# One-hots of a graph attention layer: half of them stored by the score stage and loaded back by the message stage

## The reference, cut to what matters

```python
def gt_layer(x, ntype, etype, src, dst, Wk, Wq, Wv, Wa, Watt, Wmsg, pri, skip, g, b):
    ...
    kT = jnp.einsum('nhd,htdo->nhto', k, Watt)
    vT = jnp.einsum('nhd,htdo->nhto', v, Wmsg)
    kw = kT[src, :, etype]
    m = vT[src, :, etype]
    a = jnp.einsum('ehd,ehd->eh', kw, q[dst]) * pri[:, etype].T / SQRT_D
    att = edge_softmax(a, dst, n)
    msg = (m * att[:, :, None]).reshape(-1, H * HS)
    hag = jax.ops.segment_sum(msg, dst, num_segments=n)
    ...
```

## Time and profile before

| | us |
|---|---|
| median of three executions | 5878.2 |
| the profiled execution | 5883.0 |
| its span, first to last instruction | 5881.1 |
| score stage of the first attention layer, first product store to last sum | 3807.7 to 4296.4 |
| message stage of the first attention layer, first load to last matmul | 4405.8 to 4528.7 |
| message stage of the second attention layer | 5591.0 to 5714.2 |

### The profile page before, as it was taken

The page is one execution under the profiler, slowest core; times in us unless marked ns, Lnnn a source line. Parts: engine busy times, 40 slices in busy tenths (PEclk is TensorE's granted clock), DMA queues, the critical chain, the costliest instruction groups (busy, mean ns, idle before and its releaser), DMA issues. The chain is left out here.

```text
span 5881.1 us, 64328 instructions
## 1 busy us (share of the span) xinstructions
PE 3437.1 (58%) x15913; PEld 2664.7 (45%) x15913; DVE 2302.7 (39%) x4944; ACT 1099.9 (19%) x2255; POOL 3190.0 (54%) x3405
## 2 busy tenths in 40 slices
PE   2777677767757777544654436555526265555272
PEld 2777555545546775433343322244416222444162
DVE  6222333343343334311221134444476444444774
ACT  0000222232231112000100003311116133111162
POOL 0777577667747773777377732177711320777102
PEclk9555688888875556655655567765659677565595
DMA  1222244434434333222322139955516499555162
GB/s 39 53 53 53 74 123 123 116 99 121 123 81 120 105 107 106 65 53 53 135 56 53 53 118 399 359 160 162 162 41 196 138 389 375 160 162 162 43 200 64
DMA packets 600862, 772.39 MB, mean 131 GB/s; under 512 B 89654, under 2 KB 506920, under 8 KB 587984
## 3 DMA queue, kind: packets, MB, share of 16 engines
q1 hardware_dynamic: 479920, 492.16, 25.0%
q0 software_dynamic: 120608, 276.12, 17.9%
HBM read 416.10 MB, written 351.82 MB: 131 GB/s over the span
## 5 line engine op out<-in xcount | busy, mean ns | idle before, releaser
L395 POOL DMA_INDIRECT arena<-table,idx_s x3128 | 2968.2, 949 | 1743.9 <-issue 903.0
L632 PE MATMUL ps<-arena,onehot 128*128 x4160 | 1056.8, 400 | 672.3 <-POOLq L391 638.6
L632 PEld LDWEIGHTS ps<-arena,onehot 128*128 128x128 f32 x4160 | 848.3, 284 | 807.5 <-issue 807.3
L373 DVE TENSOR_TENSOR onehot<-ps,dl_s 128x512 f32<-128x512 f32 x520 | 355.4, 685 | 813.0 <-PE ps L632 777.5
L1722 PE MATMUL ps<-ident,onehot 128*128 128x128 f32 x832 | 207.1, 396 | 438.5 <-DVE onehot L373 433.5
L1682 DVE TENSOR_TENSOR arena<-arena,ps 128x128 f32<-128x128 f32 x832 | 183.9, 282 | 560.0 <-POOLq L391 461.2
L1733 PE MATMUL ps<-arena 128*128 x1664 | 382.0, 404 | 9.4 <-issue 7.4
L802 DVE SCALAR_TENSOR_TENSOR arena<-ps,vecs,arena 128x256 f32<-128x256 f32 x208 | 100.5, 483 | 677.3 <-ACT arena L781 671.3
L1722 PEld LDWEIGHTS ps<-ident,onehot 128*128 128x128 f32 x832 | 135.5, 199 | 493.2 <-DVE onehot L373 487.4
L1733 PEld LDWEIGHTS ps<-arena 128*128 128x128 f32 x1664 | 335.8, 300 | 44.8 <-issue 40.6
L1602 PE MATMUL ps<-arena,XT 32*128 32x512 f32 x1600 | 305.0, 891 | 67.6 <-DVE XT L1626 42.8
(11 more groups left out here) (324 smaller groups left out, 4426.6 us busy)
## 6 DMA issues: line engine op xcount, KB each, us to landing
table<-arena SPq DMA_DIRECT2D x96, 2048.0 KB
values<-arena SPq DMA_DIRECT2D x832, 64.0 KB
arena<-values SPq DMA_DIRECT2D x208, 256.0 KB
arena<-table,idx_s POOLq DMA_INDIRECT x3128
arena<-edge_times SPq DMA_DIRECT2D x208, 128.0 KB, 3.4
edge_part<-arena SPq DMA_DIRECT2D x208, 128.0 KB
table<-arena SPq DMA_DIRECT2D x50, 512.0 KB
arena<-edge_part SPq DMA_DIRECT2D x98, 256.0 KB, 2.9
```

The costliest lines, as they stand in the source:

```text
L373: is_dst = dve.tensor_tensor(onehot[:, 4 * q:4 * q + 4, :], iota.unsqueeze(1).to_broadcast([P, 4, P]), dl_s[:, ds(j, 4)].unsqueeze(2).to_b ...
L395: pool.indirect_dma_start(ring[:, ds(t % RING * 2 * H, width)], None, tab, bass.IndirectOffsetOnAxis(ap=idx_s[:, t:t + 1], axis=0)).then_i ...
L632: mm = pe.matmul(accf[:, ds(b, P)], o, ring[:, ds(slot, H)], start=False, stop=False, skip_group_check=True)
```

## The change

The one-hots of the even quads (0 and 2 of each trip), which VectorE makes in the score stage anyway, are stored to a DRAM tensor `marks` there (52 stores of 256 KB per layer, in rows of 2 KB) and loaded back into the same places of `onehot` in the message stage (52 loads per layer). VectorE makes none in the message stage.

```diff
+        marks = dram("marks", [ALL_QUADS // 2, P, 4 * P])
...
+        mark_out = [signal(f"mark_out{u}") for u in range(2)]
+        mark_in = [signal(f"mark_in{u}") for u in range(2)]
...
-        def onehots(dve, weight, after=None, iota=None):
+        def onehots(dve, weight, after=None, iota=None, guard=None):
...
                     if not first:
                         dve.wait_ge(quad_done.sem, quad_done.at(n - 3))
+                        if guard is not None:
+                            guard(i, q)
...
# score_phase, SyncE
+                                if q % 2 == 0:
+                                    sp.wait_ge(onehot_ready.sem, onehot_ready.at(n + 1))
+                                    sp.dma_start(marks[n // 2, :, :], onehot[:, 4 * q:4 * q + 4, :].rearrange("p s d -> p (s d)")).then_inc(mark_out[q // 2].sem, 16)
                         trips(sp, body)
...
+                        for u in range(2):
+                            sp.wait_ge(mark_out[u].sem, mark_out[u].at(16 * TRIPS))
...
# score_phase, VectorE
+                        def kept(i, q):
+                            if q % 2 == 0:
+                                dve.wait_ge(mark_out[q // 2].sem, mark_out[q // 2].at(16 * i))
+                        onehots(dve, None, lagged, iota=ps[:, 2, 0:P], guard=kept)
...
# message_phase, SyncE
                             for q in range(QUADS):
+                                if q % 2 == 0:
+                                    if not first:
+                                        sp.wait_ge(quad_done.sem, quad_done.at(i * QUADS + q - 3))
+                                    sp.dma_start(onehot[:, 4 * q:4 * q + 4, :].rearrange("p s d -> p (s d)"),
+                                                 marks[(i * QUADS + q) // 2, :, :]).then_inc(mark_in[q // 2].sem, 16)
                                 if not first:
                                     sp.wait_ge(mixed.sem, mixed.at(i * QUADS + q - 3))
                                 sp.dma_start(vals[:, 4 * q:4 * q + 4, :],
...
# message_phase, VectorE
-                                if q % 2 == 0:
-                                    dve.tensor_tensor(onehot[:, 4 * q:4 * q + 4, :], iota_row[:, :].unsqueeze(1).to_broadcast([P, 4, P]),
-                                                      dl_s[:, ds(j, 4)].unsqueeze(2).to_broadcast([P, 4, P]), ALU.is_equal).then_inc(onehot_ready.sem, 1)
...
# message_phase, TensorE
                                 if q % 2 == 0:
-                                    pe.wait_ge(onehot_ready.sem, onehot_ready.at(i * 2 + q // 2 + 1))
+                                    pe.wait_ge(mark_in[q // 2].sem, mark_in[q // 2].at(16 * (i + 1)))
```

More of the change, by code:

```diff
@@ L1696, in lagged @@
                                 reduce(i if q >= 3 else i - 1, (q - 3) % QUADS)
-                        onehots(dve, None, lagged, iota=ps[:, 2, 0:P])
+                        def kept(i, q):
+                            if q % 2 == 0:
+                                dve.wait_ge(mark_out[q // 2].sem, mark_out[q // 2].at(16 * i))
+                        onehots(dve, None, lagged, iota=ps[:, 2, 0:P], guard=kept)
                         for q in range(QUADS - 2, QUADS):
@@ L1752, in score_phase @@
                     s.base += 64 * TRIPS
+                for s in mark_out:
+                    s.base += 16 * TRIPS
             def softmax_phase():
@@ L1921, in message_phase @@
                 mixed.base += ALL_QUADS
-                onehot_ready.base += 2 * TRIPS
                 evac.base += 2 * TRIPS
                 squared.base += HALF * TRIPS
+                for s in mark_in:
+                    s.base += 16 * TRIPS
                 for s in ring_in[0:QUADS]:
```

## The result

The changed kernel takes 5987.5 us (median of four executions, 5981.7 to 5989.3), the kernel before on the same chip 5878.4 us: a ratio of 1.0183, 95% interval 1.017 to 1.0195, so 109 us slower. Forecast were 5982 us and a range of 5922 to 6030.

What follows compares the result with a forecast made beforehand. GpSimd was taken to bound the score stage, with four nearly full resources in the message stage. A new load loop and slower clock add 101 us, score stages 3: 5878.2 + 104 = 5982 us, range 5922 to 6030.

Steps and rivals of the forecast that it cites:

- The new loop: Message stage: marks' load waits for TensorE's quad n-4 with values behind it on SyncE; 6.16 us a trip against 4.52.
- the clock: TensorE in the message stage: a fifth of the time at 1.2 GHz, lengthening the trip from 6.16 to 6.47 us.
- the sign that I had named for being wrong: Message stage: TensorE's granted clock staying 1.00 would show the forecast wrong, with 5967 us instead.
- The engines' 5.34 us: Message stage: transfer engines need 3.61 + 1.73 us a trip for values and marks; no trip can go below.
- The score stage: GpSimd's pace hides the marks' stores and VectorE's wait; only 1.4 us shows at its end, 3 us for both layers.
- rival D: Score stage: marks' stores hold up the gathers for their whole length, +89 us on top, 6071 us; 3%.
- B: Message stage: loads hidden and VectorE's relief shows, -27 us, 5851 us; 4%, half of it faster, half no change.
- A: Message stage: values land as fast as a lone load and the clock holds, 5.37 us a trip, 5925 us; 12%.
- C: Message stage: values land as a burst's fourth, a third of the time at low clock, 7.32 us a trip, 6027 us; 20%.
- VectorE's 4.12 us a trip: Message stage before the change: VectorE's work per trip, 4 x 0.689 + 2 x 0.684 us.
- That sum, 104 us: Whole kernel: 101 us from 52 longer message-stage trips and 3 us from the score stages, added to the median.

Runs made afterwards that it cites:

- The wait alone: Kernel before plus SyncE's wait for TensorE to finish quad n-4 before loading an even quad's values, no marks: 5929.2 us, ratio 1.008.
- The bytes alone: Changed kernel, but marks loaded into unread places without waiting for TensorE, and VectorE still makes the one-hots: 5919.3 us, ratio 1.0064.
- values first: Changed kernel with SyncE issuing both quads' values before the marks and their wait; slower chips: 7107.6 us, ratio 1.0099; repeated 7101.7 us, 1.0089.
- half the bytes: Changed kernel with each marks load bringing two of four matrices (128 KB), waits and order kept; slower chip: 7132.4 us, ratio 1.0124.

## Why the prediction was right

**The new loop was the right step.** Forecast were 6.16 us a trip from the loop and 6.47 with the clock; measured 6.33 and 6.51. The wait alone gave 5.40 us with no byte added, and taking the values out from behind the wait, with the same bytes, brought 5.75 and 5.72 on a queue of their own, and 5.32 when they were issued first (on the slower chips, stages alone compared).

**One term was undersized, another oversized, and they met.** The terms of the loop, forecast and taken from the trace of the changed kernel (us, means of 48 turns per stage, from the third trip on):

| term | forecast | first stage | second stage |
|---|---|---|---|
| TensorE's end to the marks' issue | 0.02 | 0.03 | 0.03 |
| marks' issue to the values' issue | 0.46 | 0.38 | 0.39 |
| values' issue until VectorE uses them | 3.60 | 3.83 | 3.88 |
| multiplication | 0.69 | 0.69 | 0.69 |
| its end until TensorE begins | 0.24 | 0.30 | 0.37 |
| a quad on TensorE | 1.15 | 1.17 | 1.23 |
| sum | 6.16 | 6.41 | 6.59 |

The loop itself was 0.25 and 0.43 us longer than forecast, most of it the load of the values. The stages hold 26 trips of 6.33 and 6.51 us, since the first trip waits for nothing, which the forecast of 52 full trips left out. The clock was put a fifth of the time at the low level, for 0.31 us a trip; it was there 2% and 12% of the time. In the first stage the granted clock was 0.99, so the sign that I had named for being wrong nearly came true there, and the trip was 6.33 us all the same. The second stage, at 0.94, is 4.8 us longer; 0.13 of its 0.18 us a turn lies in TensorE's quad and the gap before it, the terms in which the clock can show. The rows that I took the fifth from belong to other stages. That 6.47 fell beside 6.33 and 6.51 is therefore in part luck: the mechanism was right, but a clock term that was too large stood in for a landing that was too small.

**The engines' 5.34 us was a floor with the right meaning.** The bytes alone filled them to 99.9% at 5.15 us a trip, so the floor was put 0.2 us a trip too high. Neither cause gives the change by itself: 0.88 us for the wait (5.40 - 4.52), 0.63 for the bytes (5.15 - 4.52), 1.81 and 1.99 for both. Together they make more than their sum of 1.51. From the turn with the wait alone, 5.47 us, to that of the first stage, 6.41, the values take 0.71 us longer from issue to use (3.12 to 3.83) and the marks' issue adds 0.38; TensorE begins 0.17 sooner after VectorE. With half of the marks' bytes the values took 3.38 us, which speaks for the bytes as the cause of that part, though on another chip.

**The score stage was hidden, more than said.** 3 us were forecast; the traces show none, 493.5 against 493.8 us up to the next stage. On the slower chips the stores cost some 11 us a layer, but not as rival D had it: GpSimd waited 0.6 and 0.9 us for its gathers there (values first, half the bytes), and the wait for the stores was VectorE's.

**The rivals.** B needed a landing under 1.96 us; the shortest time from an even quad's issue to its use was 3.1. Relief for VectorE did not show with eight places for values and marks either, where the trip was 4.98 us. A had the clock nearly right, but the values took 1 us longer than the 2.81 of a lone load. C took 4.44 us from the fourth load of the stage, but there VectorE came straight from the third multiplication and waited for no load; the row is no landing, and 3.83 is nearer to 3.60. C's clock was wrong too. VectorE's 4.12 us a trip before the change adds up instructions that overlap in the trace: its busy time was 97.0 us in 118, 3.7 a trip. My sum does not use it. That sum, 104 us, stands against 109 by the medians and 99 by the spans.

## What to carry to other kernels

When a load gets a new wait, look at what stands behind it on its issuing queue: the wait of one small stream becomes the wait of all. Putting the stream with the tight wait on an idle engine was worth 0.6 to 0.8 us of a 6.4 us trip here, and issuing it last at least 0.6. Trading 1.4 us of a busy engine for 0.5 MB of transfers pays only where the transfer engines have that much room; here they were at 77% and the prefetch depth, not VectorE, was the cheap thing to change: four more places gave 24 and 30 us on the slower chips, 0.43 us a trip.

## What the runs showed of the hardware

With only values loaded and the transfer engines at 64%, the second of two loads of 256 KB landed 2.9 us after its issue at least and 3.3 in the median; behind a load of marks and another of values, at 84%, the median was 4.1 us. Rows of 512 bytes and of 2 KB mixed two to one reached 302 GB/s at a share of 99.9%. The granted clock of TensorE was 0.99 in a stage of 164 us in which its matmuls were busy for 110 us, and 0.94 in one of 169 us with 118 us busy, which I had not expected.
